# Attention stage of a layer with experts: values loaded for two groups of heads at a time, into a staging tile of the other arena

## The reference

```python
q, k, v = (x @ Wq.T + bq), (x @ Wk.T + bk), (x @ Wv.T + bv)      # 16 heads of 16
scores = where((j <= i) & (j >= i - 128), q k^T / 4, -10000)
ctx = (softmax(scores) + 1e-9) @ v
out = x + ctx @ Wo.T + bo + routed experts(xn) + shared expert(xn)
```

## Time and profile before

| | |
|---|---|
| median of 3 runs | 1661.37 us (1656.77 to 1661.45) |
| profiled execution | 1655.14 us, its span 1653.4 us |
| mean granted TensorE clock | 0.973 of full speed |
| busy, share of the span | PE 92%, DVE 67%, ACT 59%, POOL 67% |
| attention stage | from the first q load at 887 us to the end, 16 turns |
| chain that ended last | PE 58%, DVE 15%, ACT 10%, issue 8% |
| values' loads (line 1406) | 64 of 128 KB, 5.3 us to landing |

### The profile page before, as it was taken

The page is one execution under the profiler, slowest core; times in us unless marked ns, Lnnn a source line. Parts: engine busy times, 40 slices in busy tenths (PEclk is TensorE's granted clock), DMA queues, the critical chain, the costliest instruction groups (busy, mean ns, idle before and its releaser), DMA issues.

```text
span 1653.4 us, 38959 instructions
## 1 busy us (share of the span) xinstructions
PE 1520.1 (92%) x11382; PEld 1252.6 (76%) x11382; DVE 1105.7 (67%) x3788; ACT 979.6 (59%) x2043; POOL 1109.0 (67%) x1158
## 2 busy tenths in 40 slices
PE   4878868999999999999998899999999999999998
PEld 4766747998888999888997666677777777667766
DVE  7999875666666666666666566766666676666652
ACT  5767744454455455544554466666666666666664
POOL 1878775334433444434331488999999999999998
PEclk9999988999999999999999599999999999999999
DMA  6777755554555555545576477878877777788752
GB/s 195 269 269 269 286 195 184 170 165 156 162 165 168 160 170 164 162 138 176 164 245 149 89 155 159 178 167 174 172 173 163 163 155 164 165 168 176 168 133 88
DMA packets 228581, 288.89 MB, mean 175 GB/s; under 512 B 59488, under 2 KB 146144, under 8 KB 228512
## 3 DMA queue, kind: packets, MB, share of 16 engines
q1 hardware_dynamic: 170064, 207.30, 46.9%
q10 hardware_dynamic: 45488, 45.36, 9.6%
q0 software_dynamic: 12960, 35.41, 8.5%
HBM read 198.07 MB, written 79.95 MB: 168 GB/s over the span
## 4 chain that ended last, share of the span: by engine, by line
PE 58%; DVE 15%; ACT 10%; issue 8%; ACTq 4%; POOL 3%; DMA 2%; DVEq 0%; POOLq 0%
PE psum L152 33%; PE psum L970 11%; PE psum L1573 5%; PE psum L1531 4%; ACT plain_arena L1688 4%; PE psum L1554 2%; DVE split_arena L736 2%; PE psum L1157 2%; DVE plain_arena L1804 2%; ACTq L1707 1%; DVE stats L631 1%; ACTq L1708 1%; DVE split_arena L729 1%; ACT plain_arena L1702 1%; ACT plain_arena L1749 1%
## 5 line engine op out<-in xcount | busy, mean ns | idle before, releaser
L152 PE MATMUL psum<-split_arena 128*128 128x512 f32 (+2 forms) x4752 | 939.0, 350 | 12.3 <-DVE split_arena L1261 7.3
L152 PEld LDWEIGHTS psum<-split_arena 128*128 128x128 f32 x4752 | 750.3, 192 | 132.6 <-issue 22.9
L1804 DVE CUSTOM_DVE_ANT_0 plain_arena<-psum,mask 128x256 f32<-128x256 f32 (+1 forms) x1024 | 338.4, 385 | 198.0 <-PE psum L1531 194.2
L1688 ACT ACTIVATE plain_arena<-psum 128x512 f32<-128x512 f32 (+1 forms) x512 | 250.3, 541 | 201.7 <-PE psum L1554 171.9
L1120 POOL TENSOR_TENSOR split_arena<-plain_arena,split_arena 128x1024 fp32r<-128x1024 f32 x43 | 103.2, 2401 | 227.3 <-ACT split_arena L1192 227.0
L1226 ACT ACTIVATE plain_arena<-psum 128x512 f32<-128x512 f32 (+1 forms) x172 | 90.2, 525 | 249.7 <-PE psum L152 249.6
L970 PE MATMUL psum<-split_arena 128*128 128x256 f32 x1704 | 217.9, 286 | 3.5 <-DVE split_arena L1291 3.5
L970 PEld LDWEIGHTS psum<-split_arena 128*128 128x128 f32 x1704 | 208.0, 191 | 5.7 <-DVE split_arena L1291 4.1
L1296 DVE TENSOR_TENSOR plain_arena<-psum,plain_arena 128x512 f32<-128x512 f32 (+1 forms) x172 | 102.3, 595 | 139.9 <-ACT plain_arena L1226 137.6
L1112 POOL DMA_INDIRECT plain_arena<-xn_d,run_ix x142 | 137.1, 965 | 69.2 <-POOL run_ix L1109 35.2
L1448 POOL TENSOR_SCALAR_AFFINE_SELECT plain_arena<-plain_arena 128x1024 f32<-128x1024 f32 x128 | 140.5, 1098 | 39.5 <-ACT plain_arena L1688 38.7
(11 more groups left out here) (199 smaller groups left out, 1852.7 us busy)
## 6 DMA issues: line engine op xcount, KB each, us to landing
plain_arena<-in_gate_w SPq DMA_DIRECT2D x43, 512.0 KB, 3.4
plain_arena<-in_up_w SPq DMA_DIRECT2D x43, 512.0 KB, 4.1
plain_arena<-in_down_w SPq DMA_DIRECT2D x43, 512.0 KB, 3.4
plain_arena<-in_x SPq DMA_DIRECT2D x32, 512.0 KB, 7.0
q_d<-split_arena SPq DMA_DIRECT2D x32, 512.0 KB, 3.6
k_d<-split_arena SPq DMA_DIRECT2D x32, 512.0 KB, 5.1
split_arena<-q_d SPq DMA_DIRECT2D x128, 128.0 KB, 4.4
split_arena<-k_d SPq DMA_DIRECT2D x128, 128.0 KB, 4.8
```

What stands on the lines that cost most here:

```text
L152: last = pe.matmul(out, lhs_t(p), rhs(q), start=(begins and c == 0 and k == 0), stop=(ends and c == len(chunks) - 1 and k == 2), skip_grou ...
L1688: act.activation(b_pt[:, g % 2, 2 * p + par, 4 * half:4 * half + n, :].rearrange("p k s -> p (k s)"), psum[:, 2 + par, 0:n * P], ACT.Exp, ...
L1804: last = dve.tensor_tensor_reduce(b_junk[:, 2 * par + i % 2, 0:cols], psum[:, par, at:at + cols], mask[:, 2 * P - cols:2 * P], -1.0, 3e38, ...
```

## The change

`b_vd` moves into the split arena, read as float32, with room for two halves of a sequence's values (128 features each) in place of two groups (64 each). The old place in the plain arena stays reserved. SP loads a half at steps 7 and 15: half 0 (groups 0 and 1) and half 1 (groups 2 and 3), in runs of 512 B. The copy reads its group's 64 columns out of the half.

```diff
+        b_vd = split_take(2, T, 2 * HG * DH).bitcast(F32)
...
-        b_vd = plain_take(2, T, HG * DH)
+        plain_take(2, T, HG * DH)
...
-            def load_v(b, g):
-                s = g % 2
-                hold_after(sp, b_vc, 4 * b + g - 1)
-                sp.dma_start(b_vd[:, s, :, :], v_d[ds(b, 1), :, :, g * 64:(g + 1) * 64].rearrange(
-                    "o p a c -> p (o a) c")).then_inc(b_ldv[s], 16)
+            def load_v(b, c):
+                hold_after(sp, b_vc, 4 * (b - 1) + 2 * c + 2)
+                sp.dma_start(b_vd[:, c, :, :], v_d[ds(b, 1), :, :, c * 128:(c + 1) * 128].rearrange(
+                    "o p a c -> p (o a) c")).then_inc(b_ldv[c], 16)
...
-                    b, g = due_group(t, h, 7)
-                    if b is not None:
-                        load_v(b, g)
+                    if h in (7, 15) and valid(t):
+                        load_v(t, h // 15)
...
-                act.wait_ge(b_ldv[s], 16 * (2 * b + g // 2) + 16)
+                act.wait_ge(b_ldv[g // 2], 16 * b + 16)
                 after(act, b_pv, 4 * b + g - 1)
-                act.copy(b_v[:, s, :, :, 0].rearrange("p a c -> p (a c)"), b_vd[:, s, :, :].rearrange("p a c -> p (a c)")
+                act.copy(b_v[:, s, :, :, 0], b_vd[:, g // 2, :, s * 64:(s + 1) * 64]
                          ).then_inc(b_vc, 1)
```

## The result

The changed kernel takes 1666.72 us (median of 20 runs, 1662.02 to 1670.93) against 1661.41 for the kernel before (20 runs). The ratio is 1.0033, 95% interval 1.0022 to 1.0044: slower by 0.33%, 5.3 us. The forecast was no change (1661, with 2.1 us of loss in the sum); the time lies in the range, the sign is that of the sum, and the size is two and a half times the term.

What follows compares the result with a forecast made beforehand. TensorE and GpSimd were taken as nearly full, TensorE stalling for a transfer only at step 12. All terms were 0 but 2.1 us: 1655.14 + 2.1 = 1657.2, as a median 1661.0; 8 in 10 range 1652 to 1669.

Steps and rivals of the forecast that it cites:

- the sum: All parts of the change added up: 1655.14 us of the profiled execution + 2.1 = 1657.2 us; as a median, 1661.0.
- the term 14 x 0.3 x 0.5 = 2.1 us: Stretch behind step 7: 14 turns, 0.3 us delay of the store and maxima's load, half coming through; ends 0 and 7.1.
- the doubled load holds up the maxima: Slower rival, steps 12 and behind 15: 0.51 us a turn comes through whole, 7.1 us or up to twice; chance 0.14.
- gaps over 0.9 us in most turns: Sign at step 12 by which the rival of the doubled load holding up the maxima would be the right one.
- The delay: Behind step 7: 128 KB more hold up the store and the maxima's load behind it by 0.3 us a turn.
- my upper end: Behind step 7, if bytes limit: 128 KB / 258 GB/s = 0.51 us of delay; 7.1 us if all comes through.
- What comes through: TensorE's gap at step 12: about half reaches the end, from 0.41 of 0.86 us between two turns.
- SP's saved issues: SP's queue: 64 issues become 32, 19 us of SP's time, only lengthening its other waits: 0.
- the copy takes 426 ns: ScalarE's interleaving copy from the other arena: expected unchanged, 420 to 435 ns, effect 0.
- the DMA share of the steady stretch: DMA engines in the attention stage: from 0.79 to about 0.75, by itself worth 0.
- no gap appeared at step 4: New gaps at step 4 were a sign that the doubled load does harm.
- The rival of more room on the engines: Faster rival: store and maxima's load come free earlier, gaps of 7.4 us go; 1654.0 to 1657.7 us, chance 0.20.

## Why the prediction was wrong

The place and the mechanism held. The sum named the doubled load at step 7, the low part of the second group's maxima and the gap at step 12, and set the gap sum at 7 to 12 us; it is 13.6. What failed is the price in that sum, the term 14 x 0.3 x 0.5 = 2.1 us, where 5.3 were measured, and with it the chance of the right case, "the doubled load holds up the maxima". I put that at 0.14, mostly because its two places and 7 to 14 us seemed much. One place alone does it, and the sign that I gave for it, gaps over 0.9 us in most turns, came true (9 of 14).

- *The delay.* 0.3 us a turn, taken because twice the bytes with twice the packets cost 0.5 us on a load of q, and a longer packet was to cost less. Measured: 0.5 us in the mean landing of the low part (0.7 in the median), 0.44 us a turn in the gaps. That is my upper end, 128 KB at the 258 GB/s of that stretch, 0.51 us, and not the reduced figure. The discount for longer packets did not show: at step 7 the doubled load itself lands 0.7 us later or more. The 5.3 us in the prediction are a median over steps 7 and 15; at step 7 alone it was 5.5. The store, which the sum also took to be delayed, was not.
- *What comes through.* Half, read off one turn with a gap and one without. The right form is a threshold: the first 0.5 us is free, the rest comes through whole. The same two turns fit it as well (0.86 us of gap, 0.41 longer), and more turns would have told them apart. In the changed kernel the turns at 1231, 1276 and 1321 us take 44.66, 44.89 and 45.11 us with gaps of 0.72, 1.06 and 1.17, that is 0.3, 0.5 and 0.8 more than 44.35. A gap of before was already 0.5 us on average, so most of what was added came through: of 6.1 us more in the gap sum, the part over 0.5 us is 4.0 (3.2 before, 7.2 after). This is two thirds and not half.
- *The clock.* Not in the sum at all. A gap of 1.3 to 1.5 us was followed in some turns by a half-clock stretch, at about 1.5 us each; the profile has two in the steady turns. In the earlier trace rows the largest gap of before (1.89 us at 1011.35) was followed by one too, and I had not asked for the clock behind it. 4.0 us and two such stretches are 7 us in the profiles, more than the 5.3 between the medians. How many such stretches the timed executions had isn't shown, only that their mean clock is 0.966 to 0.972, so how the 5.3 us divide is not shown either.
- *x's load.* Not in the sum. It lands 0.8 us later, and GpSimd, which I thought had nothing to give back, waits 5.5 us for it. These waits are 1.2 us at most, and little of them can be seen in the turns; only those over 2.4 us, in other kernels, lengthened the next turn each time.
- *The rest held.* SP's saved issues brought nothing; the copy takes 426 ns; no copy waits for its load; the DMA share of the steady stretch fell from 0.79 to 0.76 (forecast 0.75); no gap appeared at step 4. The rival of more room on the engines failed where its "against" said: the room is at steps 3 and 11.

The rule of the Trainium skill that I weighed ("DMA: Bandwidth & Descriptors", section Specifications: 512 B is the smallest transfer at line rate, and below it the engine reads, modifies and writes) would have 256 KB in 512 B runs land as soon as 128 KB in 256 B runs. This nearly holds where the engines have room: 5.4 against 5.2 us at step 15, and in the kernel with the loads at steps 3 and 11 it is 4.2 against 3.8 and 5.3 against 5.7. In the full stretch at step 7 it does not, 6.2 or more against 5.5. Nor does it give the time of this kernel: with the short runs in the same places the ratio is the same within its interval.

## What to carry to other kernels

Joining two transfers saves packets, but puts the second's bytes where the first was. Look at the DMA share of that very stretch, not at its mean; where it is full, price the added bytes at the rate of that stretch, and find the small late transfer beside them that somebody waits for. A median over all issues of a line can mix places with different waits, and can leave out just the place in question; take it by place. How much of a wait reaches the end has a threshold: find what would be waited for anyway, over several turns, before taking a share of it. Ask for TensorE's clock behind its longest gaps.

## What the runs showed of the hardware

A load of 8 KB landed 1.7 us behind its issue at steps 14, 2 and 6, where the DMA share over the 4 us behind the issue was 0.31 to 0.45. Behind step 7, where that share was 1.02 before and 1.07 in the changed kernel, it took 4.4 and 5.1 us in the median, and it was hardly sooner (4.8) when no store stood ahead of it in its own queue. The mean share of the 16 engines doesn't settle it, though: with the rows at step 5 and the values at 3 and 11 the share was 0.78 and the load still took 4.3 us. Of its three landing events one came about 1 us behind the issue even in the full stretch, and the other two late; what the first one stands for isn't shown.

Gaps of 1.23 to 1.67 us on TensorE at step 12 were followed in 15 steady turns of these profiles by 3.4 us at half clock (0.51 granted), and six gaps of 1.23 to 1.44 us were not, two of them in the changed kernel (1.34 and 1.26 us). What decides between them isn't shown.
